# Context attention with heads of 32: row-max units in pairs of heads, one pair behind the scores and one behind the sums, and new places for the side work

## The reference

```python
def _mha(x, y, ...):                 # x: 16x256x128, y: context, 16x1601x64
    xn = _ln(x, lnx_g, lnx_b)
    yn = _ln(y, lny_g, lny_b)
    q = jnp.einsum('bsc,hcd->bhsd', xn, wq)
    k = jnp.einsum('btc,hcd->bhtd', yn, wk)
    v = jnp.einsum('btc,hcd->bhtd', yn, wv)
    a = jax.nn.softmax(jnp.einsum('bhsd,bhtd->bhst', q, k) * D ** (-0.5), axis=-1)
    ...
    o = jnp.einsum('bhst,bhtd->bhsd', a, v)
    o = o.transpose(0, 2, 1, 3).reshape(x.shape[0], x.shape[1], H * D)
    x_out = x + o @ li1_w + li1_b
```

## Time and profile before

| what | value |
|---|---|
| median of three runs | 8226.7 us |
| the profiled execution | 8223.36 us |
| its span | 8221.6 us |
| TensorE / VectorE / ScalarE / GpSimd busy over the span | 89% / 73% / 60% / 28% |
| the exponentials of this attention (L1277), 1792 | 869.0 us busy, 769.4 us idle before them, for the scores |
| its row-max reductions (L1357), 1536 | 1006.3 us busy, 316.6 us idle before them |
| its unit matmuls (L1160), 1536 | 523.6 us busy, 391 ns each |

### The profile page before, as it was taken

One profiled execution on the slowest core, in us unless ns is written; L12 is line 12 of the kernel. 1 busy time (PEld: TensorE's weight loads), 2 busy tenths in 40 slices (PEclk: granted clock), 3 DMA queues, 4 the chain that ended last, 5 costly groups with the idle time before them and its releaser, 6 DMA issues. The chain is left out here.

```text
span 8221.6 us, 186125 instructions
## 1 busy us (share of the span) xinstructions
PE 7300.6 (89%) x73814; PEld 3269.6 (40%) x73814; DVE 5979.8 (73%) x12917; ACT 4932.3 (60%) x9814; POOL 2317.0 (28%) x2368
## 2 busy tenths in 40 slices
PE   7999999779999996777589999999998779999979
PEld 2333333353333333344334444444444533333335
DVE  6888888648888886666556666666665458888855
ACT  4777777637888883333245555555554238888852
POOL 1222222112112200333334444545444211211200
PEclk9999999889999997777879999999999679999989
DMA  4443334124343321000100000000000134334300
GB/s 97 105 92 82 81 81 103 30 47 94 79 97 89 74 63 34 11 13 13 49 10 7 8 7 8 7 8 7 6 4 18 47 80 97 89 73 97 90 26 14
DMA packets 319827, 417.79 MB, mean 51 GB/s; under 512 B 56533, under 2 KB 238053, under 8 KB 318968
## 3 DMA queue, kind: packets, MB, share of 16 engines
q1 hardware_dynamic: 317432, 405.36, 21.7%
q10 hardware_dynamic: 1536, 0.53, 0.0%
HBM read 225.41 MB, written 174.66 MB: 49 GB/s over the span
## 5 line engine op out<-in xcount | busy, mean ns | idle before, releaser
L688 ACT ACTIVATE a_probs<-scores_ps 128x512 f32<-128x512 f32 (+2 forms) x5248 | 2818.6, 590 | 497.9 <-PE scores_ps L608 403.2
L747 DVE TENSOR_REDUCE a_unit_max<-bank 128x1 f32<-128x512 f32 x3072 | 2005.2, 683 | 195.1 <-PE bank L595 183.6
L625 PE MATMUL bank<-a_probs,a_v_sb 128*9 128x256 f32 (+1 forms) x20992 | 1617.1, 380 | 51.3 <-ACT a_out_sb L695 51.3
L608 PE MATMUL scores_ps<-a_stack 64*128 64x256 bf16 (+1 forms) x10496 | 1378.7, 274 | 14.5 <-ACT a_probs L688 9.8
L1277 ACT ACTIVATE cross_probs<-scores_ps 128x512 f32<-128x512 f32 (+1 forms) x1792 | 869.0, 571 | 769.4 <-PE scores_ps L1174 769.4
L1357 DVE TENSOR_REDUCE cross_unit_max<-bank 128x1 f32<-128x512 f32 x1536 | 1006.3, 687 | 316.6 <-PE bank L1160 312.9
L595 PE MATMUL bank<-a_stack 63*128 63x512 bf16 (+2 forms) x3413 | 1199.8, 375 | 4.8 <-DVE a_unit_max L747 1.6
L747 DVE TENSOR_REDUCE a_unit_max<-scores_ps 128x1 f32<-128x512 f32 x1536 | 1049.9, 684 | 170.7 <-PE scores_ps L595 165.4
L1444 POOL TENSOR_TENSOR cross_added<-cross_probs 128x1024 f32<-128x1024 f32 x384 | 902.3, 2350 | 942.1 <-PE bank L1207 855.3
L595 PE MATMUL scores_ps<-a_stack 63*128 63x512 bf16 (+2 forms) x1707 | 640.2, 375 | 47.2 <-DMA a_stack<-a_stack_dram 44.4
L512 POOL CAST a_parts<-a_qk 128x512 bf16<-128x512 f32 (+3 forms) x225 | 117.7, 523 | 1936.1 <-ACT a_qk L707 1852.3
(11 more groups left out here) (421 smaller groups left out, 10284.2 us busy)
## 6 DMA issues: line engine op xcount, KB each, us to landing
a_stack_dram<-a_parts SPq DMA_DIRECT2D x288, 400.2 KB, 4.3
a_stack<-a_stack_dram SPq DMA_DIRECT2D x256, 348.2 KB, 7.9
a_stack<-a_stack_dram SPq DMA_DIRECT2D x128, 444.2 KB, 10.0
a_ctxT<-in_ctxT SPq DMA_DIRECT2D x48, 400.2 KB, 4.8
a_stack_dram<-a_parts SPq DMA_DIRECT2D x288, 64.0 KB, 2.4
a_stack_dram<-a_parts SPq DMA_DIRECT2D x96, 128.0 KB, 2.4
f_x<-x_after_dram SPq DMA_DIRECT2D x32, 256.0 KB, 3.1
x_after_dram<-a_res SPq DMA_DIRECT2D x48, 128.0 KB, 4.8
```

The source lines that it names most:

```text
L608: ins = pe.matmul(score_bank[(2 * e.i + a) % 3][0:n, j * TOK + q0:(j + 1) * TOK], stack[p][rows(a, 64), 2 * e.g + j, k0:k0 + n], stack[p][ ...
L625: ins = pe.matmul(out_bank[32 * h:32 * h + V8, q0:TOK], v[0:n, e.t, 4 * e.g + h, :], A.probs[0:n, held, o + q0:o + TOK], start=(e.t == 0), ...
L688: act.activation(by_pair(A.probs[0:n, b, a * 512:(a + 1) * 512])[:, :, q0:TOK], by_pair(score_bank[(2 * e.i + a) % 3][0:n, :])[:, :, q0:TO ...
L747: ins = dve.tensor_reduce(unit_max[:, e.g % 2, qt, 2 * a + j, c:c + 1], bank[:, 0:e.s.chunks[c][1]], AX.X, ALU.max)
```

## The change

It replaces the places of the 28 units and of the side work in the cross attention. In each step there is a pair of units behind `scores` (part 0), none between `pv` and `sums` (part 1, but for two tails in step 5), and a pair behind `sums` (part 2). All seven steps of a quad get units: 4, 2, 4, 4, 4, 6, 4 from step 0 to step 6, where it was 5, 0, 5, 5, 4, 4, 5. Step 1, where the division of a quad stands, had none and has two. The tails now come before the last two full units. A `k` or `v` job now always stands between `pv` and `sums`: k c=0 in step 4, q in step 5, k c=1 in step 0 of the quad that it does not belong to, v one a step in steps 2 and 3. Before, k c=0 and c=1 were both in step 5, q in step 4, and v in steps 0.4, 1.1 (two), 1.4, 2.1 (two) and 3.1. `proj` moves from step 0.3 to 0.2; `ctx` from 2.6 and 3.0, slot 0, to 2.6, slot 2, and 3.1, slot 0; `x_turned` from 3.2 to 3.1, slot 2; one piece of `ln_stats` is one step later, the rest likewise. No instruction is added or removed in the attention. Units of the self attention with heads of 32 get the same places as before by the new rule. A unit now also waits for the cast of q, which is made after that of k c=0.

```diff
+PAIRS32 = ((-1, ((0, 0), (2, 2))), (0, ((0, 4), (2, 6))), (1, ((0, 8),)), (2, ((0, 10), (2, 12))), (3, ((0, 14), (2, 16))),
+           (4, ((0, 18), (2, 20))), (5, ((0, 24), (1, 26), (2, 22))))
...
-        for j, (i, slot) in enumerate(((4, 0), (8, 0), (8, 2), (11, 0), (15, 0), (15, 2), (22, 0))):
-            prepare(i, slot, True, "v", j=j)
+        for j, i in enumerate((3, 9, 10, 16, 17, 23, 24)):
+            prepare(i, 1, True, "v", j=j)
...
-            prepare(base - 3, 2, nxt, "q", g=g)
-            for c in range(2):
-                prepare(base - 2, 2 * c, nxt, "k", g=g, c=c)
...
+            prepare(base - 3, 1, nxt, "k", g=g, c=0)
+            prepare(base - 2, 1, nxt, "q", g=g)
+            prepare(base, 1, nxt, "k", g=g, c=1)
+            for rel, places in PAIRS32:
+                for part, first in places:
+                    for k in (first, first + 1):
+                        prepare(base + rel, 0, nxt, "unit", g=g, k=k, part=part, r=int(k == PAIRS32[-1][1][-1][1] + 1))
             prepare(base + 6, 0, nxt, "turn", g=g)
-        proj_at = (3, 2)
+        proj_at = (2, 2)
...
-        first = 1 if any(e.kind in "kv" and not s.own for e in at.get((i, 0), [])) else 2
-        plan += at.get((i, 0), []) + units[0:first]
+        by_part = [[e for e in units if e.part == part] for part in range(3)]
+        plan += at.get((i, 0), []) + by_part[0]
...
-        plan += units[first:first + 1] + at.get((i, 1), [])
+        plan += by_part[1] + at.get((i, 1), [])
...
-        plan += units[first + 1:]
+        plan += by_part[2]
...
             e.cast = cast[e.g, e.batch, "k", c // 2]
+            if not s.own:
+                e.cast = max(e.cast, cast[e.g, e.batch, "q", 0])
```

More of the change, by code:

```diff
@@ L889, in segment32 @@
             for k in range(s.NU):
-                units_at.setdefault(3, []).append(Ev("unit", k=k, r=int(k == s.NU - 1)))
+                units_at.setdefault(3, []).append(Ev("unit", k=k, part=max(k - 1, 0), r=int(k == s.NU - 1)))
             put(3, 2, "qk", g=1)
@@ L895, in segment32 @@
             for k in range(s.NU * (g > 0)):
-                prepare(g - 1, 0, True, "unit", g=g, k=k, r=int(k == s.NU - 1))
+                prepare(g - 1, 0, True, "unit", g=g, k=k, part=max(k - 1, 0), r=int(k == s.NU - 1))
             prepare(g, 0, True, "turn", g=g)
@@ L903, in segment32 @@
             for j in range(LN_PIECES):
-                put((4, 5, 11, 12, 12)[j], 1, "ln_stats", j=j)
+                put((5, 6, 12, 13, 13)[j], 1, "ln_stats", j=j)
                 put((14, 15, 16, 17, 18)[j], 2, "ln_apply", j=j)
[L906 to L909, removed]
-        for j, (i, slot) in enumerate(((4, 0), (8, 0), (8, 2), (11, 0), (15, 0), (15, 2), (22, 0))):
-            prepare(i, slot, True, "v", j=j)
+            put(13, 2, "ln_rstd")
+            put(20, 2, "ctx", j=0)
+            put(22, 0, "ctx", j=1)
+            put(22, 2, "x_turned")
+        for j, i in enumerate((3, 9, 10, 16, 17, 23, 24)):
+            prepare(i, 1, True, "v", j=j)
         for quad in range(1, QUADS + 1):
             g, base, nxt = quad % QUADS, per_quad * (quad - 1), quad == QUADS
-            prepare(base - 3, 2, nxt, "q", g=g)
-            for c in range(2):
-                prepare(base - 2, 2 * c, nxt, "k", g=g, c=c)
-            slots = [i for i, n in ((-1, 5), (0, 5), (2, 5), (3, 5), (4, 4), (5, 4)) for _ in range(n)]
-            for k in range(s.NU):
-                prepare(base + slots[k], 0, nxt, "unit", g=g, k=k, r=int(k == s.NU - 1))
+            prepare(base - 3, 1, nxt, "k", g=g, c=0)
[5 more added lines that the diff above has]
+                        prepare(base + rel, 0, nxt, "unit", g=g, k=k, part=part, r=int(k == PAIRS32[-1][1][-1][1] + 1))
             prepare(base + 6, 0, nxt, "turn", g=g)
-        proj_at = (3, 2)
+        proj_at = (2, 2)
     if with_tail:
```

## The result

The changed kernel takes 8109.4 us (median of four runs, 8103.8 to 8116.9) against 8227.1 (four runs) before: a ratio of 0.986, 95% interval 0.984 to 0.988. The direction was right, the size was not.

The account below looks back on a forecast made before the run. Steps are bound by the 3.60 us chain of scores and exponentials or by TensorE's work. Fourteen batches give -36, the last two -2 and -3.5: -41 from 8223.36, 8182, plus 3.3 makes 8186; range 8155 to 8212, wider 8132 to 8243.

Parts of the forecast that it names:

- The price of the pair behind `sums`: End of a step, ahead of the next scores: a pair with both banks free costs TensorE 0.31 us, as one alone.
- the walk: Adding up priced groups and bank returns over a batch's 28 steps: 131.7 us against 134.3, 2.6 less.
- The v job of 3.3: Between `pv` and `sums` in step 3: v adds 1.27 us, its copy returning the bank for a step of 4.87.
- The clock: Whole stage: together -41 us at an unchanged clock; the mean granted clock before was 0.98.
- (C): Rival: low-clock stretches go away with the long waits, 27 us more gained, 8160; chance 0.18.
- The new wait before the turn: Step 6: TensorE idles 1.07 us until VectorE finishes the last two full units; step 4.34, 64 x 1.07 = 68 us.
- the lone unit between `pv` and `sums`: Between `pv` and `sums`: its removal is one part of the gain; a unit alone was priced at 0.31 us.
- the k jobs behind the tails: Step 5: both k jobs gone, with the wait of 3.1 us in four; step 5 comes to 4.13.
- (A): Rival: the clock goes down; at mean 0.93, +66 us gives 8252, slower; chance 0.13.
- (B): Rival: banks bind more tightly; 0.13 us more lost in each of 20 steps a batch, 8227, no change; chance 0.17.
- (D): Rival: pairs don't run together, each 0.31 us dearer, 119 us in all, 8305; chance 0.02.
- the 0.1 a step that I allowed: Tiling-mode changes around `pv` and `sums`: a small gain in steps without a job, at most about 0.1 us each.

Follow-up runs that it names:

- ctx_back: The changed kernel with ctx and x_turned alone at their old places; 8136.5 us, 0.989 of the kernel before.
- tails_last: The changed kernel with units 22 and 23 first in step 5 and the tails last; 8069.9 us, 0.981 of the kernel before.
- pair_ahead_of_sums: The changed kernel with the pair of units 22 and 23 before `sums` in step 5; 8081.0 us, 0.982 of the kernel before.
- units_back: The changed kernel's new places of the side work, with units by the old rule; 8190.5 us, 0.996 of the kernel before.
- side_back: The changed kernel's new pairs of units, with all side work at its old places; 8187.8 us, 0.994 of the kernel before.
- step1_empty: The changed kernel with step 1's pair moved behind the other pair of step 0; 8273.1 us, 1.006 of the kernel before.
- turn_behind_pv: The changed kernel with the turn between `pv` and `sums` in step 6; 8079.8 us, 0.982 of the kernel before.
- best: The changed kernel with tails last, turn behind `pv`, ctx and x_turned earlier, statistics spread; 8032.8 us, 0.977 of the kernel before.

## Why the prediction fell short

**The price of the pair behind `sums`** is the step of the sum that failed. The prediction charged 0.31 for it, counted from the moment when its last unit can start, in every step. Where the scores follow, TensorE doesn't pay this: with both banks free the scores start 0.00 to 0.02 behind the pair (steps 5, and 3.3), and where the second unit waits for its bank they start with it, 0.15 behind the pair in steps 0 and 0.37 to 0.41 in steps 2 to 4; in steps 6 it is 0.23. The trace of before had it. In the earlier trace rows the last pair is followed by `proj`, which does come 0.07 before the pair's end, and I took that for every follower. But scores follow 22 of the 24 pairs behind `sums` in a batch. Ahead of the scores at 5004.36 stands this row:

```profile
5003.98 0.75 PE L1160 MATMUL bank<-cross_qk_b 32*128 32x512 bf16 x2
```

The scores began 0.38 behind the pair, together with its late second unit, and not 0.31 after that. In batch 5 the error reads 5.34 instead of 5.73 in steps 1.2 and 2.2, 3.97 instead of 4.13 in step 5, 4.56 instead of 4.87 in 0.3.

Alone this error would make 22 x 0.31 = 6.8 us a batch, and the batch is only 3.3 below the walk. The rest is hidden by waits that grew with it: VectorE gives the banks back no earlier, so what TensorE saves at the end of a step it waits for in the next. The timeline from 3.2 to 3.3 of batch 5 shows both:

```profile
4938.61 0.74 PE L1165 MATMUL bank<-cross_qk_b 32*128 32x512 bf16 x2
4938.98 0.80 PE L1176 MATMUL scores_ps<-cross_qk_f 32*128 32x256 f32 x8
...
4940.19 0.65 PE L1165 MATMUL bank<-cross_qk_b 32*128 32x512 bf16 x2
4940.77 1.07 PE L1203 MATMUL bank<-cross_probs,cross_v_sb 128*32 128x256 f32 x16
```

The scores start 0.37 behind the first pair, but the next pair, ahead of `pv`, takes 0.58 instead of the 0.31 charged. It is the same in 1.3, 2.3 and steps 4 (0.54 to 0.57), and the turn starts 2.07 behind the scores instead of 1.77. That these steps came out near the walk is luck: two errors of 0.3 cancel.

Three smaller terms were wrong too. The v job of 3.3 computes one tile and uses no max bank, and was charged as two: 4.37 instead of 4.87. In 3.2, 4.96 instead of 5.73, x_turned holds the scores back while VectorE goes on, so the first reduction behind the division starts 2.22 into the step and not 2.60; only 1.2 and 2.2 have the case of the walk. And the tails of step 5 took 0.39 and 0.17, not 0.2 each. ctx at the end of 2.6 costs 0.77 there, but step 3.0 falls to 4.07 (4.55 forecast). In the sum the batch is 3.3 lower, in fifteen batches 50 us of the 77 missing.

**The clock** was taken as unchanged: some 20 us. Together with the 4 us from outside the stage this leaves a few of the 77 open. Rival (C) had the direction and the size, and gave as reason that the long waits go. ctx_back doesn't bear this out: with a wait of up to 1.3 behind ctx in 14 batches the low time was smaller still, though the stretches that were left begin there. Forecast and (C) were not exclusive, and my range had room for one of them only.

**The walk by steps** was close where no cancelling is at work: step 1 3.57 (3.60 forecast), 0.2 6.31 (6.34), 3.1 4.65 (4.6). With it, it came near: steps 4 4.79 (4.87), but 3.4 5.18, steps 0 4.49, 4.65 and 5.48 (4.55, 4.70, 5.5), step 6 4.40 (4.34). The new wait before the turn is there in all quads, and it was paid in full: without most of it step 6 fell by 0.95 in tails_last and by 0.82 in pair_ahead_of_sums.

**The division of the gain** was wrong in another way. I named the lone unit between `pv` and `sums` and the k jobs behind the tails. units_back and side_back show 37 and 39 us for the halves, so a third of the gain comes from their fit. By the full batches (3.5 and some 2.0 of 5.8 us) little of that is free banks; most is the low time that units_back has and the change hasn't. Of the 81 us by which units_back is slower than the change, 33 come back with two units in step 1 (83 and 45 by the stage).

**The rivals.** (A) was wrong here and right next door: step1_empty is at a mean clock of 0.94 and slower than the kernel before. (B) happened in part: the first pairs of steps 4, 1.3 and 2.3 cost 0.23 to 0.26 more than charged and step 3.4 is 0.31 above the walk, but the price of the seam hid it. (D) is out: the pair with free banks is busy 0.38 to 0.39. On the rule of the Trainium skill about changing the tiling mode ("TensorEngine Tiling (Array Packing)", "Key Properties"): the pair of step 5 costs 0.01 ahead of the scores, which use 32 rows of the array as it does, and 0.41 between q and `sums`, which use 128, with 0.10 of it a wait. The traces agree with the rule in that, but they don't show a drain: it would look the same if matmuls on all 128 rows merely waited for the rows that the pair holds. The difference of 0.3 is more than the 0.1 a step that I allowed.

## What to carry to other kernels

The price of a small matmul group is a property of its neighbours: read it once for each follower that it will have, above all where the follower uses the array in the same tiles. A walk of the steps with bank returns got most steps right to 0.1 us, but half of an error at a seam was hidden by the waits behind it: compare the starts within a step too, and not the step's length alone. A change that fills the emptiest step of a loop can be worth more by the clock than by its own time (it was in one of the two arrangements tried), so a mean clock below 1 belongs into the forecast as a term and not as a rival. And when two kinds of work share buffers, undo each half alone before crediting either, and compare batches at the full clock, since the clock can look like their fit.

## What the runs showed of the hardware

Two matmuls of 32 rows in different row groups and different banks took 0.38 together, as one does, and the scores (32 rows) began 0.01 after such a pair in the change; ctx (128 rows) began 0.32 after it in turn_behind_pv, and `sums` (128 rows, 32 columns) 0.41 after one whose second unit was 0.10 late. The time at the lower level of the clock (1.2 GHz), without the stretch at the start, moved from nothing to 232 us of 2200 with the order of the same instructions alone. TensorE busy was 93% of the stage in the kernel before, with 92 us low, 90% in step1_empty with 232 low, and 96% in best with none, but 93% in units_back with 188: its mean does not tell.
